# Two cross-attentions and a masked audio attention on one core: the order of head pairs, of GpSimd's splits and of the audio rows, and the engine that picks the averages

## The reference

```python
def cross_attention(q_in, kv, ...):            # layers 0 and 1, with H = 16 heads of K = 128
    qh, kh, vh = q_in @ wq + bq, kv @ wk + bk, kv @ wv + bv
    kh, vh = append(kh, bias_k), append(vh, bias_v)          # one token more: 1501
    w = softmax(einsum('bqhk,bthk->bhqt', qh, kh) / sqrt(K))
    return einsum('bhqt,bthk->bqhk', w, vh) @ wo + bo
x = x + cross_attention(layer_norm(x), ctx, ...)             # layer 0
x = x + cross_attention(layer_norm(x), ctx, ...)             # layer 1
x = x + gelu(layer_norm(x) @ w_fc1 + b_fc1) @ w_fc2 + b_fc2  # 256 -> 1024 -> 256
a = layer_norm(ctx) * gamma + beta                           # audio: 16 heads of 16
scores = where(mask, (x @ Wq.T) . (a @ Wk.T) / 4, -inf)
out = x + tanh(gate) * (softmax(scores) @ (a @ Wv.T)) @ Wo.T
```

## Time and profile before

| | |
|---|---|
| runs | 1497.84, 1497.58, 1487.93 us; median 1497.58 |
| the profiled execution's own time | 1498.82 us |
| its span | 1497.1 us |
| TensorE busy | 1424.3 us (95%) |
| DVE busy | 1023.2 us (68%) |
| ACT busy | 831.6 us (56%) |
| GpSimd busy | 520.7 us (35%) |

### The profile page before, as it was taken

How to read it: one execution, slowest core, us unless ns; L and a number is a source line. 1 busy time by engine, 2 the same in 40 slices (tenths; PEclk the granted TensorE clock), 3 DMA queues, 4 the chain that set the end, 5 groups by cost and what they waited for, 6 DMA issues and landing times.

```text
span 1497.1 us, 24693 instructions
## 1 busy us (share of the span) xinstructions
PE 1424.3 (95%) x9168; PEld 893.0 (60%) x9168; DVE 1023.2 (68%) x2097; ACT 831.6 (56%) x1437; POOL 520.7 (35%) x465
## 2 busy tenths in 40 slices
PE   8799999999999998899999999999999899999986
PEld 5356666666666644366666666666554455555554
DVE  5665555555555656676665666565657899999996
ACT  4555455544455455644555444555435687777773
POOL 4533534334325100135334433430002555655400
PEclk8999999999999999999999999999999999999998
DMA  5279899898798740199888888988713799999997
GB/s 194 65 174 193 176 180 178 173 178 185 160 186 181 134 144 29 35 232 177 181 173 182 173 175 180 187 165 150 189 44 57 139 209 219 219 220 214 216 191 140
DMA packets 671795, 246.95 MB, mean 165 GB/s; under 512 B 644428, under 2 KB 645948, under 8 KB 671676
## 3 DMA queue, kind: packets, MB, share of 16 engines
q1 hardware_dynamic: 671676, 245.38, 80.5%
HBM read 85.28 MB, written 0.52 MB: 57 GB/s over the span
## 4 chain that ended last, share of the span: by engine, by line
PE 74%; DVE 16%; ACT 3%; issue 3%; DMA 3%; SPq 2%; ACTq 0%; DVEq 0%
PE SC L742 41%; PE PV L742 33%; DVE qc L1508 3%; DVE prob L1490 3%; DVE core L1549 2%; DVE qc L1417 2%; DMA core<-core 1%; DVE core L1394 1%; DVE prob L1399 1%; DVE core L1541 1%; DMA core<-qc 1%; DMA core<-in_wv_dram 1%; SPq L512 1%; ACT prob L1194 0%; ACT qc L1182 0%
## 5 line engine op out<-in xcount | busy, mean ns | idle before, releaser
L742 PE MATMUL PV<-core 128*128 128x256 f16 (+1 forms) x4800 | 540.5, 271 | 9.7 <-DMA core<-core 4.2
L742 PEld LDWEIGHTS PV<-core 128*128 128x128 f16 x4800 | 460.9, 98 | 76.9 <-issue 6.3
L1194 ACT ACTIVATE prob<-SC,core 128x500 f32<-128x500 f32 x336 | 223.9, 675 | 414.7 <-DVE core L1514 414.7
L1483 DVE TENSOR_REDUCE mx<-SC 128x1 f32<-128x500 f32 x336 | 224.3, 669 | 321.5 <-PE SC L742 321.5
L742 PE MATMUL SC<-ctxT,qc 128*128 128x500 f16 x2016 | 443.7, 374 | 0.0
L742 PEld LDWEIGHTS SC<-ctxT,qc 128*128 128x128 f16 x2016 | 195.9, 97 | 206.8
L675 POOL CAST ctxT<-stage 128x750 f16<-128x750 f32 x64 | 71.1, 1111 | 443.8 <-PE SC L742 237.6
L1541 DVE SCALAR_TENSOR_TENSOR core<-prob,core 128x1500 f16<-128x1500 f32 x112 | 194.8, 1739 | 5.7 <-ACT core L1203 5.6
L1203 ACT ACTIVATE core<-prob 128x1500 f16<-128x1500 f32 x112 | 162.7, 1453 | 3.5
L742 PE MATMUL SC<-ctxT 128*128 128x512 f16 x576 | 138.6, 384 | 8.8 <-DVE core L1549 8.7
L742 PE MATMUL SC<-qc 128*128 128x512 f16 x480 | 113.9, 382 | 18.0 <-DVE mx L1490 18.0
(11 more groups left out here) (142 smaller groups left out, 1368.6 us busy)
## 6 DMA issues: line engine op xcount, KB each, us to landing
stage<-in_ctx_nat_dram SPq DMA_DIRECT2D x64, 384.0 KB, 4.0
stage<-in_ctx_t_dram SPq DMA_DIRECT2D x64, 375.0 KB, 3.4
stage<-in_ctx_p_dram SPq DMA_DIRECT2D x32, 384.0 KB, 3.9
core<-in_wq_dram SPq DMA_DIRECT2D x8, 512.0 KB, 3.6
core<-in_wk_dram SPq DMA_DIRECT2D x8, 512.0 KB, 3.7
core<-in_wv_dram SPq DMA_DIRECT2D x8, 512.0 KB, 5.3
core<-in_wo_dram SPq DMA_DIRECT2D x8, 512.0 KB, 5.2
core<-core SPq DMA_TRANSPOSE x224, 4.1
```

Of the source, the lines that this page charges most:

```text
L742: return nc.tensor.matmul(o, a, c, start=start, stop=stop, skip_group_check=skip)
L1194: nc.scalar.activation(prob[:, i, c * CW:c * CW + w], SETS[i][c][:, 0:w], ACT.Exp, bias=nmax[:, i, :], accum_out=sum3[:, i, c:c + 1]).then ...
L1483: nc.vector.tensor_reduce(mx3[:, t % 2, c:c + 1], SETS[t % 2][c][:, 0:w], AX_X, ALU.max)\
```

## The change

What it does, engine by engine:

- GpSimd: the splits of the first context batch each wait for one more low half of the weights (`between_weights`). In the audio attention each of the four context splits and the query spreads waits for a certain tile's low half (`between_tiles`); the spreads are four instructions over all windows at once instead of 16. The mask `hm` is built in three instructions.
- TensorE: both heads' token scores are made at the odd head; each head's keys wait for its own `q_lo` alone. Four `keep_clock` matmuls stand behind the transposition at an attention's end; the counts elsewhere are changed. 8 matmuls for `vbias` are 128 columns wide, from a doubled copy of the value weights (`wv2`), and those for `obias` are gone. The output product of seven batches (`EARLY` = 392 columns) is made after the last tile's scores, and only 56 columns after the last window.
- ACT: a pick is four ACTIVATEs of 32 partitions by 56 columns, with `vbias` as their bias, between a slot's units and its exponential.
- DVE: no picks and no bias adds in the audio attention; two copies for `wv2`; the last tile of an attention takes all its maxima first; the first two low halves of the output weights come before the last scales, the other four one step later.
- The audio weights and rows are laid out head by head (32 partitions a head). `LN_UNITS` holds eight units as before, three, two and three in the norm's gaps, and none ahead of it. The result leaves by four DMAs.

```diff
-        LN_UNITS = [[0, 1], [2, 3], [4, 5], [6, 7]]
+        LN_UNITS = [[0, 1, 2], [3, 4], [5, 6, 7]]
...
+            def between_weights(n):
+
+                if n + 4 < 4 * WCH:
+                    pool.wait_ge(w_lo, 2 * W_Q[0] + n + 5)
...
+                if b >= 2:
+                    between_tiles(RT * (b - 2) + 2 + k)
...
-                pool.wait_ge(aq_lo, NW)
                 if b >= 2:
                     pool.wait_ge(as_score, RT * (b - 1))
-                for w in range(NW):
-                    for h in range(HW):
-                        c0 = OFF[w] + (HW * w + h) * Q - BASE[w]
-                        ins = nc.gpsimd.tensor_scalar(qbd[:, b % 2, :, c0:c0 + Q], qhl[:, w, :, b * Q:(b + 1) * Q],
-                                                      hm[:, h:h + 1], None, ALU.mult)
+                rows = qbd[:, b % 2, :, :].rearrange("p s (w n) -> p s w n", w=NW)
+                q = qhl[:, :, :, b * Q:(b + 1) * Q].rearrange("p w s q -> p s w q")
+                for h in range(HW):
+                    between_tiles(RT * (b - 1) + h // 2)
+                    ins = nc.gpsimd.tensor_scalar(rows[:, :, :, h * Q:(h + 1) * Q], q, hm[:, h:h + 1], None, ALU.mult)
                 ins.then_inc(qbd_ready, 1)
+
+            def between_tiles(y):
+
+                pool.wait_ge(aph_lo, max(1, y))
...
-                    if h % 2 == 0:
-                        pe.wait_ge(q_lo, H * l + h + 2)
+                    pe.wait_ge(q_lo, H * l + h + 1)
+                    if h % 2 == 1:
+                        token_score(h - 1)
                         token_score(h)
-                        token_score(h + 1)
...
+                    if h == H - 2:
+                        pe.wait_ge(q_lo, H * (l + 1))
...
                         nc.tensor.transpose(TB[0][0:TILES, 0:P], ptokc[:, :], ident[:, :]).then_inc(tok_turned, 1)
+                        keep_clock(4)
...
-                    pe.wait_ge(picked_ready, n - 1)
+                    pe.wait_ge(attn_ready, n - 1)
...
+                    if y == RT * B:
+                        for m in range(DC):
+                            early_output(m)
+
+            def early_output(m):
+
+                pe.wait_ge(attn_ready, NW * (B - 1))
+                for w in range(NW):
+                    ins = mm(TB[m][:, 0:EARLY], woa[:, w, m * P:(m + 1) * P], attnT[:, w, 0:EARLY], w == 0, w == NW - 1)
+                ins.then_inc(ew_mm, 1)
...
-                        pe.wait_ge(in_qo, 32)
                         pe.wait_ge(kv_centred, DC)
+                        pe.wait_ge(wv2_ready, 1)
                         for w in range(NW):
                             for c in range(DC):
-                                ins = mm(TB[0][0:WC, w:w + 1], kvraw[:, c, w * WC:(w + 1) * WC], col("beta", c),
-                                         c == 0, c == DC - 1)
+                                ins = mm(TB[0][:, w:w + 1], wv2[:, c, w * P:(w + 1) * P], col("beta", c), c == 0, c == DC - 1)
                         ins.then_inc(vb_mm, 1)
-                    if l == 1 and h == H - 1:
-                        pe.wait_ge(vb_ready, 1)
-                        for m in range(DC):
-                            for w in range(NW):
-                                ins = mm(TB[0][:, m:m + 1], woa[0:WC, w, m * P:(m + 1) * P], vbias[:, w:w + 1],
-                                         w == 0, w == NW - 1)
-                        ins.then_inc(ob_mm, 1)
...
-            keep_clock(10)
-            layer_norm(0, lambda at: keep_clock((4, 2, 5)[at]))
+            keep_clock(7)
+            layer_norm(0, lambda at: keep_clock((5, 4, 6)[at]))
...
-                    ins = mm(S[m][:, 0:NQ], woa[:, w, m * P:(m + 1) * P], attnT[:, w, :], w == 0, w == NW - 1)
+                    ins = mm((M, S[0])[m][:, 0:Q], woa[:, w, m * P:(m + 1) * P], attnT[:, w, EARLY:NQ], w == 0, w == NW - 1)
...
-                            act.wait_ge(qp_mm, DC * (H * l + h - 3))
+                            act.wait_ge(qp_mm, DC * (H * l + h - 3) + 1 - h % 2)
...
-                    if h == H - 1:
+                    if h == H:
                         act.wait_ge(tok_scores, l + 1)
...
+            def pick_average(b, w):
+
+                n = NW * b + w
+                act.wait_ge(apv_done, n + 1)
+                for h in range(HW):
+                    own = slice(2 * KA * h, 2 * KA * (h + 1))
+                    ins = nc.scalar.activation(attnT[own, w, b * Q:(b + 1) * Q], PV[w % 2][own, h * Q:(h + 1) * Q],
+                                               ACT.Identity, scale=1.0 / PROB_SCALE, bias=vbias[own, w:w + 1])
+                ins.then_inc(attn_ready, 1)
...
+                        for c in range(DC):
+                            ins = nc.vector.tensor_copy(
+                                wv2[:, c, :].rearrange("p (h s k) -> p h s k", h=H, s=2),
+                                kvraw[:, c, 0:D].rearrange("p (h k) -> p h k", h=H).unsqueeze(2).broadcast_to([P, H, 2, KA]))
+                        ins.then_inc(wv2_ready, 1)
...
-            def pick_average(b, w):
-
-                n = NW * b + w
-                dve.wait_ge(apv_done, n + 1)
-                nc.vector.tensor_tensor(picked[:, w % 2, :, :], PV[w % 2][:, 0:WR].rearrange("p (h q) -> p h q", h=HW),
-                                        hms[:, :].unsqueeze(2).broadcast_to([P, HW, Q]), ALU.mult).then_inc(picked_ready, 1)
-                dve.wait_ge(picked_ready, n + 1)
-                nc.vector.tensor_reduce(attnT[:, w, b * Q:(b + 1) * Q], picked[:, w % 2, :, :].rearrange("p h q -> p q h"),
-                                        AX_X, ALU.add).then_inc(attn_ready, 1)
...
-                    if x == 1:
+                    if x in (1, TILES - 1):
                         maximum(t, 1)
                         maximum(t, 2)
                         row_maximum(t)
@@ -1597,11 +1617,14 @@
                         total(t - 1)
                         probs_low(t - 1)
                         inverse(t - 1)
-                    if x < TILES and x != 1:
+                    if x == TILES:
+                        for i in range(2):
+                            weights_low(2 * W_O[l] + i)
+                    if x < TILES and x not in (1, TILES - 1):
                         maximum(t, 1)
                     if 1 <= x <= TILES:
                         scales(t - 1)
-                    if x < TILES and x != 1:
+                    if x < TILES and x not in (1, TILES - 1):
                         maximum(t, 2)
...
-                    if x >= TILES and x < TILES + LAG:
-                        for i in ((0, 1), (2, 3, 4, 5))[x - TILES]:
+                    if x == TILES + LAG - 1:
+                        for i in range(2, 6):
...
+                    if y == RT * B:
+                        add_audio(TB, ew_mm, 0, EARLY)
...
-                    if y == 1:
-                        dve.wait_ge(ob_ready, 1)
-                        dve.wait_ge(tg_ready, 1)
-                        dve.wait_ge(aq_mm, NW)
-                        nc.vector.tensor_scalar(obias[:, :], obias[:, :], tg[:, 1:2], None, ALU.mult).then_inc(xb_ready, 1)
-                    if y == 2:
-                        dve.wait_ge(xb_ready, 1)
-                        for c in range(DC):
-                            nc.vector.tensor_scalar(xT[:, c, :], xT[:, c, :], obias[:, c:c + 1], None, ALU.add)\
-                                .then_inc(xb_ready, 1)
```

124 lines of the change are left out of this document (59 added, 65 removed).

## The result

The changed kernel takes 1483.11 us (median of 17 runs), the kernel before 1495.86 (17 runs): ratio 0.9924, interval 0.9909 to 0.9938, so 9 to 14 us faster. The forecast was 1470, with a range of 1455 to 1484; the range was just reached, but less than half of the 28 us came, and the time stayed 0.5 above the 1482.6 under which the prediction spoke of faster.

The account below looks back on a forecast made before the run. The chain was 74% TensorE and 16% DVE, with DVE bounding the audio attention. Terms 3.5 + 11.1 - 3.5 + 2.0 + 10.6 + 4.6 = 28.3 off 1498.8 gave 1470 us, range 1455 to 1484.

Parts of the forecast that it names:

- Audio: Audio attention: with picks off DVE, TensorE bounds a batch at 39.3 us instead of 40.67; 10.6 us gained.
- Rival (1): Audio period stays at 40.7, held by the transposition queue or ACT's line; 10.6 becomes 2, total 1479; chance 0.20.
- Start: Before the first product: holding GpSimd shortens two pairs of DVE low halves; 3.8 less 0.3 for the clock, 3.5 gained.
- Head pairs: Query projections: keys fill waits before token scores, a pair takes 5.3 us; 8.9 gained in layer 0, 6.6 in layer 1.
- Token row: After the last head pair: the row's transfer starts about 2.4 us later, TensorE waits some 2.7; -2.2 a layer.
- Ends: Both attention ends: all maxima first delays a low half, its transposition and the output heads; -3.5 us, between -5 and +1.5.
- Last norm: Around the last layer norm: bias records go and two units move into gaps; +2.0 us, between -1 and +4.6.
- Tail: After the last pick: four small matmuls and short adds, 1.1 us instead of 5.75; 4.6 gained.
- Rival (4): Audio attention: an ACT pick instruction costs more than 0.70 us, ACT bounds the batch; slower, 1509 at 0.8; chance 0.04.

Follow-up runs that it names:

- e4: Changed kernel, the transposition of the probabilities' low halves moving 6 of 12 column blocks from the second audio batch on: 1472.01 us, ratio 0.9839.
- e5: Changed kernel, audio context loads bringing a third of their columns from the third batch on, with as many DMA instructions: 1472.62 us.
- e3: Changed kernel with a pick as one ACTIVATE of 128 partitions by 56 columns instead of four of 32: 1478.31 us.
- e11: Changed kernel with early last-pair token scores and DVE's old order at attention ends, GpSimd's first context splits not waiting for weights' low halves: 1475.15 us.
- e1: Changed kernel with the last head pair's token scores made ahead of head 14's keys again: 1476.79 us, ratio 0.9872.
- e12: Changed kernel with early last-pair token scores and DVE's old order at attention ends, without the four fill matmuls there: 1474.5 us.
- e2: Changed kernel with DVE's order at an attention's end as before the change, fills kept: 1480.25 us, ratio 0.9904.
- e9: Changed kernel with early last-pair token scores and DVE's old order at attention ends, norm units three, three, two: 1469.07 us, ratio 0.9809.

## Why the prediction went wrong, point by point

- **Audio, forecast 10.6, measured 2.1: the step that failed.** It was the pair "TensorE is the bound with 38.45" and, of SyncE's waits, "even all of it gone leaves its queue busy or blocked 38.0 a batch, under TensorE". The removal itself was sized right: DVE fell to 178.94 / 5 = 35.8 (35.2 forecast), ACT rose to 36.2 (35.4), and TensorE's floor exists (38.7 in e4 and e5). But the waits do not go, and the rest is no constant: SyncE's DMA instructions held its queue 38.3 us of the batch before and 39.1 of the 40.95 in the changed kernel, and only with fewer bytes in flight does the batch fall to TensorE (e4, e5). The very row that the sum used shows a DMA share of 1.14 in batches 1 to 5, the highest in the earlier trace rows. Rival (1) had the right time for this part (2 of 10.6) and named the transposition queue or ACT's line. Of ACT's line e3 leaves at most 1 us a batch. The queue is indeed full, but it is the bytes that fill it (e5), not the number of its instructions. That the stage gained 2.1 at all is within the spread of its executions; the first batch, where the share is 0.91, gained its 3.1 (2.8 forecast), and batches 1 to 5 lost 1.4.
- **Start, 3.5 forecast, 4.4 measured,** and 4.4 by e11, each from two executions of a stage that spreads by 2 us. The cause was right: the pairs went from 3.17 and 3.23 to 1.3 each. Two terms were missing: the bias scalings between the pairs, also stretched beside GpSimd (1.00 before, 2.42 in e11, 0.40 with the hold), and the clock, where the 0.3 taken off had the wrong sign: the hold also spares it.
- **Head pairs, 15.5 forecast before the token row, 13.9 measured** (8.1 and 5.8). The chain was read rightly; a pair's work is 5.5, the upper of the two bounds, not 5.3 (from 564.20 to 569.71 in layer 1's timeline, where nothing waits). The lower bound took the idle time of the weight loads, 2.53, off the 7.68; the matmuls themselves stood 2.12 there, and 0.84 in the plain pairs where the prediction has 1.25.
- **Token row, -2.2 a layer forecast;** the waits grew by 1.9 and 2.3. Missed was what an idle TensorE can cost behind it: 3.4 us of low clock in layer 1, nothing in layer 0 of this execution. That the range had no term for it is the second error by size. e1 removes both.
- **Ends, -3.5 forecast, about -1 measured:** +1.9 in layer 0 (the fills and the clock, e12), -2.9 in layer 1 (2.4 for the maxima's order, e2, and 0.5 for the fills, e12). The mechanism was the one described; its price in layer 0 was too high, since TensorE waits there for the weights' halves in any case (e2).
- **Last norm, +2.0 forecast, -0.5 measured** (between 1.5 and -2.6 in the eleven executions with this order of units). The removed 2.5 and the faster units came; they went to unit 7, which waits 3.0 for DVE in all of them, and here to the clock of what follows. The forecast had moved units into gaps as if each gap could take any number; e9 shows that the order of three, three, two keeps 2.6 to 4.
- **Tail, 4.6 forecast, 4.7 measured.** The picks are 0.3 longer than said, the adds as short.
- Against the reference time: the forecast was made from an execution of 1498.8, and the median of 17 runs before is 1495.86, so 3 of the 13 us between 1470 and 1483 are the starting point.

Rival (4), the slower one, needed 0.70 us an ACTIVATE; it is 0.296, and ACT had room for it.
